# Values stored as fp32 rows and picked by an fp32 product, in place of an fp16 high and low pair

## The reference, cut to what matters

```python
x = x + L0(_gn(x), w0, w1, w2, bias)    # three-level Haar wavelet convolution, 5x5, 128 to 128 channels
x = x + L1(_gn(x), spatial_weight)      # local similarity filter, below

def L1(x, spatial_weight):              # x is the normalised image, 5x5 neighbourhoods
    patches = _extract_patches(x)                                # [b, c, 25, h, w]
    dot = einsum('bchw,bckhw->bkhw', x, patches)
    norm_x, norm_p = sqrt(sum(x * x, axis=1)), sqrt(sum(patches * patches, axis=1))
    sim = dot / maximum(norm_x[:, None] * norm_p, EPS)
    weight = (sim + 1) * 0.5 * spatial_weight[None, :, None, None]
    return einsum('bckhw,bkhw->bchw', patches, weight)
```

## Time and profile before

| what | value |
|---|---|
| median of 3 runs | 2229.93 us (2226.68 to 2234.81) |
| the profiled execution | 2236.67 us, its span 2235.0 us |
| mean granted TensorE clock in it | 0.829 |
| TensorE busy: products, weight loads | 1634.4 us, 862.5 us |
| VectorE busy | 1408.0 us |
| ScalarE busy, GpSimd busy | 738.2 us, 448.3 us |
| the chain that ended last, by engine | TensorE 27%, DMA 21%, VectorE 18%, SyncE's queue 17%, issue 11% |

### The profile page before, as it was taken

How to read it: one execution, slowest core, us unless ns; L and a number is a source line. 1 busy time by engine, 2 the same in 40 slices (tenths; PEclk the granted TensorE clock), 3 DMA queues, 4 the chain that set the end, 5 groups by cost and what they waited for, 6 DMA issues and landing times.

```text
span 2235.0 us, 49426 instructions
## 1 busy us (share of the span) xinstructions
PE 1634.4 (73%) x16895; PEld 862.5 (39%) x16895; DVE 1408.0 (63%) x2121; ACT 738.2 (33%) x1222; POOL 448.3 (20%) x792
## 2 busy tenths in 40 slices
PE   5777777878578776888568785778678795875465
PEld 3543333434234343434234342335334352432243
DVE  6428646966378455966478554866479554875354
ACT  2321233423243233424233242423334242423341
POOL 1352422022301222012300232013300232011000
PEclk7888888989789897979788896989888896887566
DMA  5242446763857546673856556583766557572665
GB/s 164 75 125 75 122 129 152 185 171 92 192 141 192 140 126 167 157 186 99 189 149 183 134 133 167 140 207 99 172 162 174 139 131 178 139 197 76 146 164 135
DMA packets 151106, 329.95 MB, mean 148 GB/s; under 512 B 47092, under 2 KB 96244, under 8 KB 150260
## 3 DMA queue, kind: packets, MB, share of 16 engines
q1 hardware_dynamic: 109296, 207.18, 37.2%
q0 software_dynamic: 41472, 118.24, 20.1%
HBM read 238.70 MB, written 86.61 MB: 146 GB/s over the span
## 4 chain that ended last, share of the span: by engine, by line
PE 27%; DMA 21%; DVE 18%; SPq 17%; issue 11%; ACT 3%; DVEq 2%; POOL 0%; ACTq 0%; POOLq 0%
DMA d_n<-st_n 12%; PE conv L1300 8%; PE conv L1274 5%; DMA unit_mem<-d_n 5%; SPq L385 4%; DMA unit_mem<-d_hl 3%; SPq L413 3%; PE gram L1368 3%; PE conv L1259 3%; SPq L383 2%; PE out_ps L1393 2%; SPq L408 2%; SPq L405 2%; DVE wgt L1020 2%; PE stat_ps L1323 2%
## 5 line engine op out<-in xcount | busy, mean ns | idle before, releaser
L1020 DVE SCALAR_TENSOR_TENSOR wgt<-gram,tapw 124x512 f32<-124x512 f32 x512 | 350.4, 687 | 360.5 <-PE gram L1368 321.9
L1300 PE MATMUL conv<-thl,wconv 128*128 128x496 f16 (+2 forms) x1920 | 559.9, 422 | 16.8 <-DVE xa L899 9.6
L471 POOL DMA_DIRECT2D ring<-in_x x576 | 333.7, 584 | 475.3 <-DVE bn L781 244.1
L1368 PE MATMUL gram<-unit_mem 128*60 128x128 f16 x4096 | 264.8, 255 | 198.9 <-DMA unit_mem<-d_hl 122.8
L1368 PEld LDWEIGHTS gram<-unit_mem 128*60 128x60 f16 x4096 | 160.6, 118 | 428.9 <-issue 427.2
L1323 PE MATMUL stat_ps<-st_n,sq_c 128*128 128x306 f32 x256 | 123.0, 570 | 186.7 <-ACT st_n L556 153.7
L1300 PEld LDWEIGHTS conv<-thl,wconv 128*128 128x128 f16 x1920 | 171.2, 105 | 223.8 <-issue 81.3
L1274 PE MATMUL conv<-thl,wconv 128*128 128x480 f16 (+7 forms) x1200 | 255.3, 367 | 0.0
L1393 PE MATMUL out_ps<-wgt,vals 124*32 124x128 f32 x4096 | 195.2, 311 | 35.6 <-issue 31.5
L556 ACT ACTIVATE vals<-vals_ps 124x512 f32<-124x512 f32 x128 | 76.3, 596 | 391.5 <-PE vals_ps L1351 391.5
L505 POOL DMA_DIRECT2D up<-d_z x128 | 68.7, 539 | 560.4 <-DVE xa L951 500.5
(11 more groups left out here) (133 smaller groups left out, 2007.3 us busy)
## 6 DMA issues: line engine op xcount, KB each, us to landing
unit_mem<-d_hl SPq DMA_DIRECT2D x128, 360.0 KB, 6.5
unit_mem<-d_hl SPq DMA_DIRECT2D x256, 180.0 KB, 8.4
ring<-in_x POOLq DMA_DIRECT2D x288, 128.0 KB, 4.1
ring<-in_x POOLq DMA_DIRECT2D x288, 127.0 KB, 4.4
d_hl<-st_hl SPq DMA_DIRECT2D x128, 180.0 KB
d_v<-st_v SPq DMA_DIRECT2D x128, 180.0 KB
unit_mem<-d_v SPq DMA_DIRECT2D x64, 360.0 KB
up<-d_z POOLq DMA_DIRECT2D x160, 128.0 KB, 3.2
```

The costliest lines, as they stand in the source:

```text
L471: pool.dma_start(dst, src).then_inc(raw_in[slot], 16)
L1020: V.scalar_tensor_tensor(out=dst, in0=g, scalar=SIM_SCALE ** 2, in1=tapw[:, :].unsqueeze(1).to_broadcast([KN, 2, 2 * QN]), op0=ALU.add, op ...
L1300: last = mm(dst[:, :, b0:b1], wconv0[:, w, 2 * (p % ROWS4) + s, dx + 2, :], thl[:, p % 2, d, s, :, b0 + dx:b1 + dx] if p % ROWS4 != 1 else ...
L1368: last = mm(bank[row:row + KQ, col:col + QN], key[:, q, e_at, TH * KW * g:TH * KW * g + KQ], tile[:, :, TH * g + 1:TH * g + 1 + TH, 1:1 + ...
```

## The change

Values are kept in fp32. ScalarE's copy of the strips writes fp32 and is all that is done to them: `value_lows` and its semaphore are gone, and `unit_lows` waits for the copy (`v_kept`) instead. SyncE saves them by one DMA of 360 KB in place of two of 180 KB. On the way back the values of a unit are loaded by two DMAs: rows 0 to 31 hold quadrants 0 and 1, rows 32 to 63 hold quadrants 2 and 3, each row 1440 fp32 elements, which is as many bytes as before. The product takes 64 rows of fp32, of which half belong to another quadrant; `pick_c[:, q // 2]` has zeros for these and a one over the scale for the wanted ones. The number of products and their shapes stay, the operands are fp32. The counts of the two semaphores follow: five to four DMAs on a save, five to six on `rest_in`.

```diff
-SAVES, LOADS, LATER = 80, 96, 80
+SAVES, LOADS, LATER = 64, 96, 96
...
-    unpair = np.zeros((2 * C, C), np.float16)
-    unpair[np.arange(2 * C), np.arange(2 * C) % C] = 1 / X_SCALE
+    pick = np.zeros((2 * C, 2, C), np.float32)
+    pick[np.arange(2 * C), np.arange(2 * C) // C, np.arange(2 * C) % C] = 1 / X_SCALE
...
-        st_v = sb("st_v", [P, 2, 2, FN], F16)
+        st_v = sb("st_v", [P, 2, FN], F32)
...
-        unpair_c = sb("unpair_c", [2 * C, C], F16)
+        pick_c = sb("pick_c", [2 * C, 2, C], F32)
...
-        keys, queries, values = ([unit_part(s, n) for s in range(2)] for n in range(3))
+        keys, queries = ([unit_part(s, n) for s in range(2)] for n in range(2))
+
+        values = [unit_mem[:, s, 2 * Q * FN:3 * Q * FN].bitcast(F32).rearrange("p (q e n) -> p q e n", q=2, e=GROUPS) for s in range(2)]
...
-        d_v = dram("d_v", [B, 2 * BANDS, 2, C, Q, FN], F16)
+        d_v = dram("d_v", [B, 2 * BANDS, C, Q, FN], F32)
...
-                for hl in range(2):
-                    sp.dma_start(d_v[b, h, hl].rearrange("c q n -> q c n"), st_v[:, hl, h % 2, :]).then_inc(half_saved[h % 2], 16)
+                sp.dma_start(d_v[b, h].rearrange("c q n -> q c n"), st_v[:, h % 2, :]).then_inc(half_saved[h % 2], 16)
...
-                sp.dma_start(values[s][0:2 * C].rearrange("c q e n -> c (q e n)"),
-                             d_v[b, u].rearrange("l c q n -> (l c) (q n)")).then_inc(rest_in[s], 16)
+                for t in range(2):
+                    sp.dma_start(values[s][C * t:C * t + C].rearrange("c q e n -> c (q e n)"),
+                                 d_v[b, u, :, 2 * t:2 * t + 2, :].rearrange("c q n -> c (q n)")).then_inc(rest_in[s], 16)
...
-                copy(in_strips(st_v[:, 0, half, :]), strips(part)).then_inc(v_high, 1)
+                copy(in_strips(st_v[:, half, :]), strips(part)).then_inc(v_kept, 1)
...
-            def value_lows(b, h):
-                dve.wait_ge(v_high, 8 * b + h + 1)
-                V.tensor_tensor(in_strips(st_v[:, 1, h % 2, :]), strips(image_of(h)), in_strips(st_v[:, 0, h % 2, :]),
-                                ALU.subtract).then_inc(value_low, 1)
-
             def unit_lows(b, h):
                 dve.wait_ge(unit_high, 8 * b + h + 1)
-                dve.wait_ge(value_low, 8 * b + h + 1)
+                dve.wait_ge(v_kept, 8 * b + h + 1)
...
-                    value_lows(b, h)
...
-                                if k == 0:
-                                    value_lows(b, h)
...
-                                      values[s][0:2 * C, q, e, TH * KW * g:TH * KW * g + KQ], unpair_c[:, :],
+                                      values[s][0:2 * C, q % 2, e, TH * KW * g:TH * KW * g + KQ], pick_c[:, q // 2, :],
```

More of the change, by code:

```diff
@@ L130, in host_constants @@
             taps[64 * (k % 2):64 * (k % 2) + KQ, t, k // 2] = (dr == t // K - K // 2) & (dc == t % K - K // 2)
-    return square, gather, taps.reshape(KN, TAPS * 2 * QN), unpair
+    return square, gather, taps.reshape(KN, TAPS * 2 * QN), pick
 def first(n):
@@ L153, in link, with build @@
         engine.wait_ge(self.sem, self.base + self.k)
-def build(nc, x, w0, w1, w2, bias, spatial, square, gather, tapmask, unpair, out):
+def build(nc, x, w0, w1, w2, bias, spatial, square, gather, tapmask, pick, out):
     ctx = ExitStack()
@@ L298, in build @@
         sq_done = sem("sq_done")
-        v_high = sem("v_high")
+        v_kept = sem("v_kept")
         n2_ready = sem("n2_ready")
@@ L306, in build @@
         unit_high = sem("unit_high")
-        value_low = sem("value_low")
         unit_low = sem("unit_low")
@@ L372, in _ @@
             sp.dma_start(spat[:, :], spatial.rearrange("(a k) -> a k", a=1).to_broadcast([P, TAPS])).then_inc(const_in, 16)
-            sp.dma_start(unpair_c[:, :], unpair).then_inc(const_in, 16)
+            sp.dma_start(pick_c[:, :, :], pick).then_inc(const_in, 16)
             sp.wait_ge(wmixed, 7)
@@ L1542, in const_arrays @@
 def const_arrays():
-    return dict(zip(("square", "gather", "taps", "unpair"), host_constants()))
+    return dict(zip(("square", "gather", "taps", "pick"), host_constants()))
 _INS = ["x", "L0_conv_w0", "L0_conv_w1", "L0_conv_w2", "L0_conv_bias", "L1_conv_spatial_weight"]
```

## The result

The changed kernel takes 2306.3 us, median of 4 runs (2294.2 to 2323.9), against 2231.9 us (2226.7 to 2234.8) before: a ratio of 1.034, 95% interval 1.025 to 1.043. It is slower by 74 us.

What follows compares the result with a forecast made beforehand. No engine alone bounds it: VectorE, TensorE and a load path in S1 to S4, DMA in S5 and run-up, TensorE after. Seven rounds at +9.4 give 66, last image +5: +71 on 2236.7, 2308, median 2301; range 2225 to 2370.

Steps and rivals of the forecast that it cites:

- Batch: The 32 value products of one hook: 2.0 us in fp32, +1.42 at the full clock, +2.35 at the lower.
- Rival (B): Value products: weight loads of successive fp32 products do not overlap, 3.2 us a batch, +180, 2410 us; chance 0.12.
- Units 6 and 7: End of a full round, from the end of S5: four batches with TensorE alone, +6.6 us a round.
- S5, S6 and S7: Last three of seven stretches between a round's results: DMA sets the first, TensorE alone the other two.
- S1 to S4: First four stretches between a round's results, VectorE and TensorE both nearly full: together +3.3 us a round.
- Run-up: Rest of a round outside the seven stretches, 118.7 us, ending in DMA: run-up and DMA -0.5 us a round.
- Bytes against rows: Saves: if engine time goes by bytes, nothing is gained; if by rows, a quarter, 2.8 us. Bytes was favoured.
- Last image: The image without convolution: TensorE freer, only its four last batches counted, +5 us.
- (A): Rival: fp32 records keep their present pace and VectorE ends S1 to S4, -11, 2219 us; chance 0.12.
- (C): Rival, no change: saves go by rows, not bytes, 67 us off against +71, 2234 us; chance 0.08.
- (D): Rival: load path holds S1 to S4, hiding the added work wholly, +48, 2278 us; forecast with it 0.65.

Runs made afterwards that it cites:

- e1: Kernel before with its 4096 value products alone turned to fp32, saves, loads and VectorE's low part kept: 2315.2 us, 1.040.
- e2: Changed kernel with its saves, loads and VectorE work, but the value products in fp16: 2197.7 us, 0.986.
- e3: Kernel before without VectorE's operation that makes the low part of the values; saves, loads and products stay: 2220.6 us, 0.996.
- e9: e2 with the values saved by two DMAs of 1440-byte rows again, in place of one of 2880-byte rows: 2219.7 us, 0.996.
- e4: Kernel before with each fp16 value product issued twice: 2284.9 us, 1.023.
- e6: Changed kernel with the quadrant ahead of the channel in memory, so saves go as 128 rows and loads gather shorter rows: 2122.6 us, 0.949.
- e5: Changed kernel with one wide fp32 product for both quadrants of a row block, 16 products a batch in place of 32: 2221.2 us, 0.993.

## Why the prediction was right, point by point

The forecast was 2301 us, the result 2306. The mechanism held: the fp32 product doubles the records, each load is slower, and this lands where TensorE is alone. That the sum came within 5 us is partly luck. Two terms were wrong in opposite directions, and the profiles that the terms are read from differ by 58 us where the sum had 71.

- **Batch.** 2.0 us forecast, 1.88 measured; at the lower clock +2.35 forecast, 3.34 less 0.96 = +2.38 measured. The count of records was exact. Rival (B), loads one after another, would have shown 3.2 us. A record every 29 ns with 47 ns of columns means that the loads of successive records overlap; that it takes the turn between the two output halves is not shown, since no run leaves it out. The Trainium skill's rule (TensorE: Matmul & The Clock Gate, "The mechanism") that a load overlaps running products only where the row groups differ does not describe these products, which all read rows 0 to 63.
- **Units 6 and 7.** +6.6 forecast; S5, S6 and S7 grew by 3.4, 2.2 and 1.3, +6.9. S6 and S7 fit (3 x 1.30 = 3.9, measured 3.5). In S5 the agreement hides two things that the forecast had not: the product alone gives +3.8 there (e1) where 2.35 was counted, and the rest of the change alone -2.4 (e2).
- **S1 to S4.** +3.3 forecast, +2.1 measured, but not where I put it: S2, where idle time was to hide the work, grew by 1.4, and S1 and S3 did not. With VectorE's operation left in (e1), the four grow by 2.6; the operation is worth 9 us in all (e3). Idle time per stretch does not tell which of the waits between two nearly full engines end last.
- **Run-up, the step that failed.** "The save has one issue less, 0.7 us" was true of save 0 only. In saves 1 and 2 the issue is held up behind a load and takes up to 8.5 us, which the trace of before shows (7.44 us for the two at L385) and the prediction did not use. I took 0.5 us a round, within bounds of +1.5 to -8.4; it is -2.8 in the profiles and 22 us of the whole by e9 against e2. Bytes against rows was answered rightly for a lone save, and was the wrong question for those behind a load; save 1 landed 2.1 us sooner after the change and save 2 3.9 sooner, of which e3 has 2.6 without any change of the saves. The Trainium skill's rule that the number of engines is the largest up to 16 that divides the slowest dimension of both sides (DMA: Bandwidth & Descriptors, "Why a DMA increments its semaphore by 16 and not by 1") is borne out: the window of save 0 moves 98 GB/s at a share of 0.32 with a slowest dimension of 4, and 205 at 0.54 with one of 128.
- **Last image, the other step that failed.** +5 forecast, +15.6 measured: +4.0 in its run-up, +2.1 in S1 to S4, +9.5 in S5 to S7. "TensorE freer" overlooked its clock, and "only its four last batches" the twelve others, three of which lie in the run-up. The rows are S6 of the last image before, after, and in e1:

```profile
2210.63:2221.34 10.71, 8.38 (x196) 5.82 (x195) 6.02 (x11) 1.93 (x3) 0.00 (x0) 0.82 0.42 107
```

```profile
2260.47:2276.96 16.49, 14.85 (x256) 12.23 (x256) 5.90 (x11) 2.43 (x3) 0.00 (x0) 0.50 0.25 68
```

```profile
2284.18:2297.06 12.88, 10.44 (x256) 8.38 (x256) 5.85 (x12) 2.44 (x3) 0.00 (x0) 0.83 0.32 86
```

Without convolution the engine is often idle and spends much of the time at the lower level of 1.2 GHz: over the last image its granted clock is 0.59 both before and after. Nine of the 16 batches after the change ran wholly at it, 3.34 us each, among them the four last, which took 0.96, 0.59, 0.89 and 0.96 us before: +10 us, where S5 to S7 grew by 9.5. That was not bound to happen: with the same product, e1 had the full clock in most of S6 and S7 (0.83 and 1.00), and these two grew by only 1.3 us there, against 8.1. The whole last image grew by 11.5 in e1.
- **(A)** fell with the batch. A cheaper pass would indeed have made the kernel faster: e2 is at -32.
- **(C) and (D).** (C) gave the saves 67 us; e9 against e2 gives them 22, and not by the rows of a lone save. (D) had the work hidden in S1 to S4, where the forecast had +3.3; they grew by 2.1 us.
- **Left open.** The product alone is +85, the rest alone -32, together 53, while the change measured +74 (56 to 96 by its interval). By their own intervals the two parts allow 40 to 74, so whether they add is open. And the changed kernel's runs spread over 1.3%, those before over 0.4%; no run explains that.

## What to carry to other kernels

An fp32 product here is twice the records, each loading its columns at less than half the speed (47 ns against 21 for 60 columns); where the streamed side is short, the load is the price, so widen the streamed side. Read what a DMA issue takes where it stands: 0.6 us with nothing ahead of it, up to 8.5 behind a load. And before trimming a transfer look at its DMA share: at 0.27 to 0.32 about a quarter of the engines carried the saves, and another order in memory was worth 184 us, more than the change itself.

## What was not expected of the hardware

- Twice as many TensorE instructions in a batch bring idle time inside batches: 70 us over 32 batches in e4, with the same shapes and data, each pause ending 1.3 to 1.8 us after a packet of the instruction queue.
- The same bytes in rows of 1440 and 2880 bytes in place of 5760 did not slow the loads: in e6 the keys and queries, all in DMAs of 180 KB, landed in a median of 5.0 us, against 7.1 for the queries (180 KB) and 5.7 for the keys (360 KB) in the changed kernel.
- About a third of what the batches grew by reaches the end, whichever way they grow: the 128 batches together (start to the next operation) went from 90 to 329 us in e1 for +85 us, and to 243 us in e4 for +55; from 87 us in e2 to 158 in e5 it is +23.
